# Layer two of a graph block: the edge rows are scaled by one VectorE product a batch, in place of sixteen ScalarE scalings

## The chip, the cores and the metric

One core of one Trainium2 chip runs the whole program. A core has five engines, each with an instruction stream of its own: TensorE (PE), VectorE (DVE), ScalarE (ACT), GpSimd (POOL) and SyncE (SP). They meet through semaphores only. The metric is the device time of one execution, in microseconds (us).

## The reference

A block on 6250 nodes with 256 features: two layers of graph attention over 106250 edges, a linear attention beside them, and a mixture of eight experts behind. What matters here is the second graph layer, and what follows it:

```python
def gat_conv(x, W, attn_l, attn_r, src, dst, n_nodes):     # layer two: H = 1, D = 256
    feat = (x @ W).reshape(n_nodes, H, D)
    e = jax.nn.leaky_relu(el[src] + er[dst], NEG_SLOPE)
    m = jax.ops.segment_max(e, dst, num_segments=n_nodes)
    ex = jnp.exp(e - m[dst])
    denom = jax.ops.segment_sum(ex, dst, num_segments=n_nodes)
    alpha = ex / denom[dst]
    return jax.ops.segment_sum(alpha[:, :, None] * feat[src], dst, num_segments=n_nodes)
...
    h = jnp.einsum('bfd,edh->bfeh', x, W1) + b1             # eight experts, three layers each
    h = jax.nn.relu(_bn(h, g1, be1, m1, v1))
    h = jnp.einsum('bfeh,ehk->bfek', h, W2) + b2
    h = jax.nn.relu(_bn(h, g2, be2, m2, v2))
    y = jnp.einsum('bfeh,ehd->bfed', h, Wo) + bo
    return jnp.einsum('bfed,fe->bfd', y, w)
```

Each edge's source row `feat[src]` is multiplied by a weight `ex` of its own and added to the sum of its destination.

## The kernel before

The program runs five passes: nodes, indices, the edges of layer one (with the linear attention beside them), the hidden pass between the layers, and the edges of layer two (with the experts beside them). The functions are the same for both layers; a `Layer` gives the numbers. Layer two has one head (`H` = 1) of 256 columns (`W` = `dim` = 256).

**Edges.** They are sorted by destination and laid out on 128 lanes. A *row* is one edge on each lane; 16 rows (`G`) are a *batch*, and a layer has 52 batches (`NB`). `rows` holds three batches in layer two: for each row 256 features, and in column `W` the score, later the weight.
- GpSimd gathers: one indirect DMA a row (`e_rows<-scratch_table,k_src`, L1349). It may write batch n only when the same row of batch n - 3 has been summed (`summed`).
- VectorE's `head(n + 1)` (L1399 to L1418) makes the score differences `d` of the next batch. It stands in batch n's code ahead of row 14, and needs all 16 gathers of batch n + 1.
- ScalarE takes the exp of `d` into `wr` (L1473) and into column `W` of `rows` (L1474), both at the start of batch n's code, behind everything it does in batch n - 1. Then it scales row after row in place (L1481) and signals each (`scaled`).
- VectorE sums: L1437 and L1441 for row 0, L1458 for rows 1 to 15, each on the one before (`ring`). In L1458 both the row and the running sum are inputs. Half batches of `ring` are stored by SyncE.

**Experts.** Work on nodes, four blocks of 121 at a time, is woven into the same code by the batch and the row: four batches are a *round*, and in it TensorE takes its group of nodes through the eight experts, two a batch. For expert e its program has the first layer of e + 1 (L2090, into `p_a`), the second of e (L2102, into `p_b`), the outputs of e - 1 (L2116, into `p_y`). ScalarE empties `p_a` and `p_b` into `h1`, `h2` by L2025, which stands in its code at rows 2, 5, 9 and 12 of a batch (in the fourth batch of a round partly at 8, 10 and 13). VectorE adds `p_y` to `y` by L1878 at rows 1 and 2 for one expert and at rows 8 and 9 for the next; TensorE's outputs of an expert wait until those of the expert before it have been added. In the first batch of a round VectorE also runs the scans of the tails (L1129, L1132) at row 3, for which TensorE waits with L1138; in its third it joins the sums of a finished group (from L1898 on; the shares and the first join at row 7, behind ScalarE's exp L2062).

Layer one has eight heads; ScalarE scales four of them, and VectorE the other four in one product a batch (L1427), 128 x 16 x 256 elements too, whose weights a copy of the exps in PSUM gives (`shared`). Layer two fills all of PSUM with the experts' banks and the tails' and has no `shared`.

Of the kernel before, what the change touches and what calls it, by code (L numbers as in the profile page):

```python
# [8 lines left out]
ALU = mybir.AluOpType  # L9
# [3 lines left out]
P = 128  # L13
# [6 lines left out]
G = 16  # L20
# [39 lines left out]


L1 = Layer("l1", 8, 512, 4, 2, 12)
L2 = Layer("l2", 1, 256, 1, 3, 14)


def wait(eng, sem, value):
# [1192 lines left out]
def edge_pass(nc, a, k, L, work_of):  # L1259
    H, W, R, dim, AH = L.heads, L.width, L.row, L.dim, L.act_heads  # L1260
# [3 lines left out]
    with Scope(nc, "e" + L.name[1]) as s:  # L1264
# [5 lines left out]
        rows = s.sb("rows", [P, B, G, L.table])  # L1270
# [13 lines left out]
        scaled, summed = s.sem("scaled"), s.sem("summed")  # L1284
# [1 line left out]
        stored = s.sems("stored")  # L1286
        tails = Tails(nc, a, k, L, s, tails_out)
        work = work_of(nc, a, k, s, tails, stored)
        shared = [s.ps(f"shared{i}", [P, 512]) for i in range(2)] if AH < H else None
        shared_ready = s.sem("shared_ready")  # L1290

        def share(b):
# [63 lines left out]
        def _(dve):  # L1356
            c = Steps(dve, step)
# [63 lines left out]
            for n in range(NB):  # L1421
                b, rb = n % 2, n % B
                dve.wait_ge(wr_ready, n + 1)
                if AH < H:
                    dve.wait_ge(shared_ready, n + 1)
                    v = rows[:, rb, :, AH * dim:W].rearrange("p j (h e) -> p j h e", h=H - AH)
                    c(nc.vector.tensor_tensor(v, v, broad(share(b)[:, AH:H, 1:G1].rearrange("p h j -> p j h"), dim), ALU.mult))  # L1427

                wait(dve, stored[0], n * 16)
                wait(dve, summed, n * G)  # L1430
                if AH < H:
                    c(nc.vector.tensor_tensor(ring[:, 0, 0, 0:W].rearrange(by_head, h=H),
                                              ring[:, 1, LENGTH[1] - 1, 0:W].rearrange(by_head, h=H),
                                              broad(share(b)[:, :, 0], dim), ALU.mult))
                    c(nc.vector.tensor_tensor(ring[:, 0, 0, W:W + H], ring[:, 1, LENGTH[1] - 1, W:W + H], wr[:, b, :], ALU.mult))
                else:
                    c(nc.vector.tensor_scalar(ring[:, 0, 0, 0:W + H], ring[:, 1, LENGTH[1] - 1, 0:W + H], wr[:, b, 0:1], None,  # L1437
                                              ALU.mult))
                c.done()
                dve.wait_ge(scaled, n * G + 1)  # L1440
                nc.vector.tensor_tensor(ring[:, 0, 0, 0:W + H], ring[:, 0, 0, 0:W + H], rows[:, rb, 0, 0:W + H], ALU.add  # L1441
                                        ).then_inc(summed, 1)

                for i, (c0, c1) in enumerate(HALVES):
                    if i == 1:
                        wait(dve, stored[1], n * 16)
                    for j in range(max(c0, 1), c1):
                        if j == L.ahead and n < NB - 1:
                            head(n + 1)
                        er_along(n, j)  # L1450
                        tails.vector(dve, n, j)
                        work.vector(dve, n, j)
                        if j == G - 1 and n:
                            wait(dve, tails.kept, n // PB)
                        prev = ring[:, i, j - c0 - 1, 0:W + H] if j > c0 else ring[:, 1 - i, LENGTH[1 - i] - 1, 0:W + H]
                        dve.wait_ge(scaled, n * G + (j + 1))
                        dve.wait_ge(summed, n * G + j)
                        nc.vector.scalar_tensor_tensor(ring[:, i, j - c0, 0:W + H], prev, k.same[:, n * G + j:n * G + j + 1],  # L1458
                                                       rows[:, rb, j, 0:W + H], ALU.mult, ALU.add).then_inc(summed, 1)
# [3 lines left out]
        def _(act):  # L1463
            work.scalar_first(act)
            act.wait_ge(er_ready, 1)
            for n in range(NB):
                b, rb = n % 2, n % B
                act.wait_ge(d_ready, n + 1)
                wait(act, summed, (n - 1) * G)
                if AH < H:  # L1470
                    nc.scalar.activation(shared[b][:, 0:H * G1], d[:, :, :].rearrange("p h j -> p (h j)"), ACT.Exp  # L1471
                                         ).then_inc(shared_ready, 1)
                nc.scalar.activation(wr[:, b, :], d[:, :, 0], ACT.Exp).then_inc(carry_ready, 1)  # L1473
# [3 lines left out]
                for i, (c0, c1) in enumerate(HALVES):  # L1477
                    for j in range(c0, c1):
                        for h in range(AH):
                            at = slice(h * dim, (h + 1) * dim)  # L1480
                            last = nc.scalar.activation(rows[:, rb, j, at], rows[:, rb, j, at], ACT.Copy,  # L1481
                                                        scale=rows[:, rb, j, W + h:W + h + 1])
                        last.then_inc(scaled, 1)
                        tails.scalar(act, n, j)
                        work.scalar(act, n, j)
                    wait(act, stored[i], n * 16)
                    nc.scalar.copy(ring[:, i, 0:c1 - c0, L.max:R],
                                   mext[:, b, :, 1 + c0:1 + c1].rearrange("p h j -> p j h")).then_inc(dm_ready[i], 1)
# [794 lines left out]
```

## Time and profile before

| | us |
|---|---|
| median of three timed runs | 3574.6 (3569.72 to 3576.8) |
| the profiled execution, its time | 3602.09 |
| its span, from the first instruction to the last | 3600.3 |
| mean granted TensorE clock over the span | 0.752 of full |

The profile is of one execution. The page gives, for each engine, its busy time over the span; the trace behind it gives every instruction with its start, its length, how long the engine had stood idle before it, and what ended that idle time. Layer two's batches run from 1987.7 us to the end of the gathers and sums near 3423; from then on TensorE works off the last experts.

### The profile page before, as it was taken

The page shows a single profiled execution, that of the slowest core. Times are in us where ns is not written, and L with a number is a line of the kernel's source. Part 1 is how long each engine was busy: PE and PEld are TensorE (multiplying, and loading weights), DVE is VectorE, ACT ScalarE, POOL GpSimd, SP SyncE. Part 2 cuts the span into 40 slices and gives each one's busy share as a digit, 9 for nine tenths or more (in the row PEclk, how much of TensorE's full clock was granted, in tenths as well). Part 3 has the DMA queues.
Part 4 walks back from the last instruction along what each step waited for, and adds up shares of the span by engine and source line. Part 5 has one row for each costly group of instructions (what it writes and reads, how often), then busy time and mean ns, then how long its engine had stood idle before and what let it go on. Part 6 is the DMA issues. An engine that isn't in the chain of part 4 may idle for free. (4 is left out here: it accounts for less than half of the span.)

```text
span 3600.3 us, 33860 instructions
## 1 busy us (share of the span) xinstructions
PE 2150.5 (60%) x7289; PEld 1354.6 (38%) x7289; DVE 2346.6 (65%) x5584; ACT 1911.7 (53%) x6229; POOL 2178.0 (60%) x2067
## 2 busy tenths in 40 slices
PE   6700555554554444443664004788888878878999
PEld 5600333332332333332443002444554445544565
DVE  6872788887888888786775244555565545655732
ACT  3301888787877767675443223544554445544632
POOL 2337677666777767673775766666666666666300
PEclk9855667666656655555887556899989989989999
DMA  6414899998999999996554475555555555555410
GB/s 219 125 21 121 324 359 351 338 334 329 353 351 375 361 327 371 333 373 247 152 142 99 142 234 166 161 170 183 188 159 170 178 165 184 171 159 181 151 36 12
DMA packets 249058, 793.62 MB, mean 220 GB/s; under 512 B 72064, under 2 KB 120035, under 8 KB 222197
## 3 DMA queue, kind: packets, MB, share of 16 engines
q0 software_dynamic: 132448, 379.32, 33.9%
q1 hardware_dynamic: 86327, 391.15, 28.6%
q10 hardware_dynamic: 30078, 20.99, 2.3%
q8 instruction: 59, 0.97, 0.1%
q14 instruction: 146, 1.20, 0.1%
HBM read 414.03 MB, written 378.16 MB: 220 GB/s over the span
## 5 line engine op out<-in xcount | busy, mean ns | idle before, releaser
L1349 POOL DMA_INDIRECT e_rows<-scratch_table,k_src x1664 | 1745.1, 1049 | 837.4 <-issue 397.8
L1458 DVE SCALAR_TENSOR_TENSOR e_ring<-e_ring,k_same,e_rows 128x520 f32<-128x520 f32 (+1 forms) x1560 | 968.0, 621 | 458.5 <-ACT e_rows L1481 177.0
L1481 ACT ACTIVATE e_rows<-e_rows 128x64 f32<-128x64 f32 (+1 forms) x4160 | 1199.8, 373 | 35.0 <-issue 29.9
L2116 PE MATMUL e_p_y<-e_wfo,e_h 128*121 128x256 f32 x1664 | 414.4, 404 | 135.3 <-DVE e_y L1878 117.4
L2116 PEld LDWEIGHTS e_p_y<-e_wfo,e_h 128*121 128x121 f32 x1664 | 323.4, 197 | 242.0 <-issue 124.2
L2090 PE MATMUL e_p_a<-e_xt,e_wf 128*128 128x484 f32 x832 | 383.9, 607 | 22.5 <-ACT e_xt L2040 11.7
L2025 ACT ACTIVATE e_h<-e_p_a,e_shift,e_scale 128x484 f32<-128x484 f32 x208 | 151.7, 750 | 448.1 <-remote 295.0
L1878 DVE SCALAR_TENSOR_TENSOR e_y<-e_p_y,e_w,e_y 121x256 f32<-121x256 f32 x416 | 181.3, 478 | 304.2 <-remote 105.9
L2102 PE MATMUL e_p_b<-e_h,e_wf 128*128 128x484 f32 x832 | 360.0, 572 | 7.9 <-issue 7.4
L1427 DVE TENSOR_TENSOR e_rows<-e_rows,e_shared 128x4096 f32<-128x4096 f32 x52 | 229.7, 4418 | 18.7 <-ACT e_shared L1471 7.5
L971 PE MATMUL e_p_kv<-e_wkv,nd_feat 128*121 128x512 f32 x208 | 184.6, 1039 | 92.0 <-DVE nd_feat L876 62.8
L2090 PEld LDWEIGHTS e_p_a<-e_xt,e_wf 128*128 128x128 f32 x832 | 168.7, 205 | 186.4 <-issue 160.6
L2025 ACT ACTIVATE e_h<-e_p_b,e_shift,e_scale 128x484 f32<-128x484 f32 x208 | 151.2, 749 | 148.4 <-PE e_p_b L2102 66.2
L2102 PEld LDWEIGHTS e_p_b<-e_h,e_wf 128*128 128x128 f32 x832 | 153.1, 190 | 176.5 <-issue 171.6
L1007 PE MATMUL e_p_q<-k_ident,e_low 121*128 121x121 f32 x104 | 33.1, 418 | 294.1 <-DVE e_low L902 253.1
L985 PE MATMUL e_p_c<-e_vext,e_kphi 121*128 121x129 f32 x208 | 62.5, 394 | 191.8 <-ACT e_low L938 99.9
L1123 PE MATMUL e_p_x<-k_ident,e_fin 128*8 128x128 f32 (+1 forms) x26 | 8.1, 313 | 203.9 <-ACT e_fin L1118 197.1
L1473 ACT ACTIVATE e_wr<-e_d 128x8 f32<-128x8 f32 (+1 forms) x104 | 21.4, 205 | 204.1 <-DVE e_d L1418 98.7
L1007 PEld LDWEIGHTS e_p_q<-k_ident,e_low 121*128 121x128 f32 x104 | 15.7, 207 | 299.3 <-DVE e_low L902 256.4
L1675 PE MATMUL hi_p_f<-hi_w,hi_ht 128*121 128x272 f32 x416 | 122.4, 445 | 0.1
L985 PEld LDWEIGHTS e_p_c<-e_vext,e_kphi 121*128 121x128 f32 x208 | 44.7, 266 | 200.3 <-ACT e_low L938 106.6
L971 PEld LDWEIGHTS e_p_kv<-e_wkv,nd_feat 128*121 128x121 f32 x208 | 57.9, 308 | 159.0 <-issue 87.1
(405 smaller groups left out, 3589.8 us busy)
## 6 DMA issues: line engine op xcount, KB each, us to landing
scratch_sums<-e_ring SPq DMA_DIRECT2D x104, 2112.0 KB
scratch_sums<-e_ring SPq DMA_DIRECT2D x104, 1032.0 KB
e_rows<-scratch_table,k_src POOLq DMA_INDIRECT x1664
scratch_table<-na_frow ACTq DMA_DIRECT2D x52, 245.8 KB
scratch_table<-hi_frow ACTq DMA_DIRECT2D x52, 124.8 KB
na_x<-in_x SPq DMA_DIRECT2D x13, 484.0 KB
e_wkv<-in_x SPq DMA_DIRECT2D x52, 121.0 KB
scratch_res<-e_wkv SPq DMA_DIRECT2D x52, 121.0 KB
```

The costliest lines, as they stand in the source:

```text
L971: nc.tensor.matmul(self.p_kv[0:BK, :], self.k.feat[:, t, kt, :], self.wkv[:, kt, :], start=kt == 0, stop=kt == 1)
L985: last = nc.tensor.matmul(self.p_c[:, m * (P + 1):(m + 1) * (P + 1)], part[0:BK, m * P:(m + 1) * P], self.vext[:, m, :], start=False, stop ...
L1349: nc.gpsimd.indirect_dma_start(out=rows[:, n % B, g, :], out_offset=None, in_=table, in_offset=bass.IndirectOffsetOnAxis(ap=k.src[:, n * G ...
L1427: c(nc.vector.tensor_tensor(v, v, broad(share(b)[:, AH:H, 1:G1].rearrange("p h j -> p j h"), dim), ALU.mult))
L1458: nc.vector.scalar_tensor_tensor(ring[:, i, j - c0, 0:W + H], prev, k.same[:, n * G + j:n * G + j + 1], rows[:, rb, j, 0:W + H], ALU.mult, ...
L1481: last = nc.scalar.activation(rows[:, rb, j, at], rows[:, rb, j, at], ACT.Copy, scale=rows[:, rb, j, W + h:W + h + 1])
L1675: last = nc.tensor.matmul(p_f[b][0:BK, 0:D + 16], ht[:, b, kt, :], w2[:, kt, :], start=kt == 0, stop=kt == 3)
L1878: last = nc.vector.scalar_tensor_tensor(y, self.p_y[bank][0:BK, i % 2 * D:(i % 2 + 1) * D], self.w[:, i, e:e + 1], y, ALU.mult, ALU.add)
L2025: self.nc.scalar.activation(h[:, e % 2, mt, :], p[mt][:, 0:GN], ACT.Relu, bias=self.shift[:, layer, 2 * e + mt:2 * e + mt + 1], scale=self ...
L2090: last = nc.tensor.matmul(self.p_a[mt][:, 0:GN], self.wf1[:, e, kt, mt * P:(mt + 1) * P], self.xt[:, kt, :], start=kt == 0, stop=kt == 1)
L2102: last = nc.tensor.matmul(self.p_b[mt][:, 0:GN], self.wf2[:, e, kt, mt * P:(mt + 1) * P], self.h1[:, e % 2, kt, :], start=kt == 0, stop=kt ...
L2116: last = nc.tensor.matmul(self.p_y[bank][0:BK, i * D:(i + 1) * D], self.h2[:, e % 2, kt, v:v + BK], self.wfo[:, e, kt, :], start=kt == 0, ...
```

## The change

`act_heads` of layer two goes from 1 to 0. The branch for it scales a whole batch with one TENSOR_TENSOR on VectorE, all 16 x 256 columns of a lane, whose second operand is the weight column of the same tile, repeated over 256 columns. It reads both operands in SBUF and stands at the head of the batch, behind the wait for the exps. ScalarE has no scaling and signals none, and VectorE's waits for `scaled` are gone. `shared` stays out in layer two, and layer one is as before.

```diff
-L2 = Layer("l2", 1, 256, 1, 3, 14)
+L2 = Layer("l2", 1, 256, 0, 3, 14)
...
-        shared = [s.ps(f"shared{i}", [P, 512]) for i in range(2)] if AH < H else None
+        shared = [s.ps(f"shared{i}", [P, 512]) for i in range(2)] if 0 < AH < H else None
...
                 dve.wait_ge(wr_ready, n + 1)
-                if AH < H:
+                if AH == 0:
+                    c(nc.vector.tensor_tensor(rows[:, rb, :, 0:W], rows[:, rb, :, 0:W], rows[:, rb, :, W:W + 1].to_broadcast([P, G, W]),
+                                              ALU.mult))
+                elif AH < H:
                     dve.wait_ge(shared_ready, n + 1)
...
-                if AH < H:
+                if 0 < AH < H:
                     c(nc.vector.tensor_tensor(ring[:, 0, 0, 0:W].rearrange(by_head, h=H),
...
                 c.done()
-                dve.wait_ge(scaled, n * G + 1)
+                if AH:
+                    dve.wait_ge(scaled, n * G + 1)
...
-                        dve.wait_ge(scaled, n * G + (j + 1))
+                        if AH:
+                            dve.wait_ge(scaled, n * G + (j + 1))
...
-                if AH < H:
+                if 0 < AH < H:
                     nc.scalar.activation(shared[b][:, 0:H * G1], d[:, :, :].rearrange("p h j -> p (h j)"), ACT.Exp
...
-                        last.then_inc(scaled, 1)
+                        if AH:
+                            last.then_inc(scaled, 1)
```

In VectorE's stream, at the passage from the first to the second batch of a round (batches 32 and 33), the program had these rows before: the last of `head`, the last two sums of the batch, then row 0 of the next (L1437, L1441) and the adds to `y`.

```order
3523 L1417 TENSOR_TENSOR e_d<-e_eext,e_mext 128x1
3524 L1418 TENSOR_TENSOR e_d<-e_eext,e_mext 128x16
3525 L1458 SCALAR_TENSOR_TENSOR e_ring<-e_ring,k_same,e_rows 128x257 x2
3526 L1437 TENSOR_SCALAR e_ring<-e_ring,e_wr 128x257
3527 L1441 TENSOR_TENSOR e_ring<-e_ring,e_rows 128x257
3528 L1878 SCALAR_TENSOR_TENSOR e_y<-e_p_y,e_w,e_y 121x256 x2
3529 L1458 SCALAR_TENSOR_TENSOR e_ring<-e_ring,k_same,e_rows 128x257
```

After the change the same place reads as follows, with the line numbers of the changed file (L1463 is the sum, L1440 and L1445 row 0, L1884 the add to `y`).

```order
3556 L1417 TENSOR_TENSOR e_d<-e_eext,e_mext 128x1
3557 L1418 TENSOR_TENSOR e_d<-e_eext,e_mext 128x16
3558 L1463 SCALAR_TENSOR_TENSOR e_ring<-e_ring,k_same,e_rows 128x257 x2
3559 L1425 TENSOR_TENSOR e_rows<-e_rows 128x16x256
3560 L1440 TENSOR_SCALAR e_ring<-e_ring,e_wr 128x257
3561 L1445 TENSOR_TENSOR e_ring<-e_ring,e_rows 128x257
3562 L1884 SCALAR_TENSOR_TENSOR e_y<-e_p_y,e_w,e_y 121x256 x2
```

One row is new, the product L1425, ahead of row 0's sum and the adds; nothing else changes its place.

ScalarE's stream at the same passage before: the end of batch 32 with its scalings (L1481) between the banks (L2025), then the exps of batch 33 (L1473, L1474).

```order
2226 L1487 COPY e_ring<-e_mext 128x8
2227 L1481 ACTIVATE e_rows<-e_rows 128x256 x2
2228 L2025 ACTIVATE e_h<-e_p_a,e_shift,e_scale 128x484 x2
2229 L1481 ACTIVATE e_rows<-e_rows 128x256 x3
2230 L2025 ACTIVATE e_h<-e_p_b,e_shift,e_scale 128x484 x2
2231 L1481 ACTIVATE e_rows<-e_rows 128x256 x3
2232 L1487 COPY e_ring<-e_mext 128x8
2233 L1473 ACTIVATE e_wr<-e_d 128x1
2234 L1474 ACTIVATE e_rows<-e_d 128x16
```

And after the change (L2031 empties a bank, L1478 and L1479 are the exps):

```order
2013 L1493 COPY e_ring<-e_mext 128x8
2014 L2031 ACTIVATE e_h<-e_p_a,e_shift,e_scale 128x484 x2
2015 L2031 ACTIVATE e_h<-e_p_b,e_shift,e_scale 128x484 x2
2016 L1493 COPY e_ring<-e_mext 128x8
2017 L1478 ACTIVATE e_wr<-e_d 128x1
2018 L1479 ACTIVATE e_rows<-e_d 128x16
```

The scalings are gone, and the exps follow the last bank behind one small copy.

## Rows read from the trace of the kernel before

**Rows 1.** The page: span, and busy time of each engine.

```profile
span 3600.3 us, 33860 instructions
PE 2150.5 (60%) x7289; PEld 1354.6 (38%) x7289; DVE 2346.6 (65%) x5584; ACT 1911.7 (53%) x6229; POOL 2178.0 (60%) x2067
```

**Rows 2.** Table of stretches: batches 0-7, 12-47, 48 to end; columns as headed.

```profile
core 0: us, PE busy (x) PEld busy (x) DVE busy (x) ACT busy (x) POOL busy (x), PEclk, DMA share, GB/s
1987.70:2213.20 225.50, 15.38 (x48) 9.07 (x49) 86.39 (x259) 63.21 (x174) 156.48 (x157) 0.51 0.58 185
2330.60:3338.90 1008.30, 838.37 (x2639) 493.75 (x2639) 572.12 (x1738) 501.69 (x1126) 653.34 (x657) 0.90 0.56 173
3338.90:3600.30 261.40, 251.38 (x842) 152.04 (x840) 111.38 (x317) 106.31 (x198) 33.41 (x33) 0.99 0.20 65
```

**Rows 3.** Groups, 2330.6 to 3338.9: busy us, mean ns | idle before <-releasers.

```profile
L1349 POOL DMA_INDIRECT e_rows<-scratch_table,k_src x577 | 569.5, 987 | 330.9 <-DVE e_ring L1458 167.1 <-issue 154.0 <-DVE e_ring L1441 8.6
...
L1138 PE MATMUL e_p_x<-k_ident,e_chain 1*128 1x1 f32 x9 | 2.0, 222 | 5.3 <-DVE e_chain L1132 5.3
```

**Rows 4.** Timeline in layer one: start, us, engine, instruction [idle before <-releaser].

```profile
597.46 4.42 DVE L1427 TENSOR_TENSOR e_rows<-e_rows,e_shared 128x4096 f32<-128x4096 f32 x1
598.56 0.95 POOL L1349 DMA_INDIRECT e_rows<-scratch_table,k_src  x1 [0.30 <-issue]
599.81 0.95 POOL L1349 DMA_INDIRECT e_rows<-scratch_table,k_src  x1 [0.30 <-issue]
```

**Rows 5.** Who waited for whom, 2330.6 to 3338.9: us, times, longest.

```profile
ACT e_h L2025 <- remote: 300.2, 52, 22.2
...
DVE e_ring L1458 <- ACT e_rows L1481: 103.3, 64, 9.4
PE e_p_y L2116 <- DVE e_y L1878: 102.4, 19, 15.2
```

**Rows 6.** Timeline, third batch of a round (batch 34), three engines.

```profile
2930.53 3.41 PE L2090 MATMUL e_p_a<-e_xt,e_wf 128*128 128x484 f32 x8
...
2952.51 0.95 POOL L1349 DMA_INDIRECT e_rows<-scratch_table,k_src  x1 [0.30 <-issue]
2956.89 1.40 ACT L2025 ACTIVATE e_h<-e_p_a,e_shift,e_scale 128x484 f32<-128x484 f32 x2 [22.23 <-remote]
...
2959.47 1.14 POOL L1349 DMA_INDIRECT e_rows<-scratch_table,k_src  x1 [6.01 <-DVE e_ring L1458]
```

**Rows 7.** Timeline, passage from a round's first to its second batch (32 to 33).

```profile
2910.57 1.40 ACT L2025 ACTIVATE e_h<-e_p_b,e_shift,e_scale 128x484 f32<-128x484 f32 x2 [6.39 <-remote]
2911.86 1.30 ACT L1481 ACTIVATE e_rows<-e_rows 128x256 f32<-128x256 f32 x3
...
2914.30 0.21 ACT L1474 ACTIVATE e_rows<-e_d 128x16 f32<-128x16 f32 x1
...
2915.58 0.94 POOL L1349 DMA_INDIRECT e_rows<-scratch_table,k_src  x1 [1.48 <-DVE e_ring L1458]
...
2916.05 0.87 DVE L1878 SCALAR_TENSOR_TENSOR e_y<-e_p_y,e_w,e_y 121x256 f32<-121x256 f32 x2
...
2917.06 1.31 PE L2116 MATMUL e_p_y<-e_wfo,e_h 128*121 128x256 f32 x5 [0.59 <-DVE e_y L1878]
```

**Rows 8.** Timeline of VectorE in batch 0 of layer two, two sums.

```profile
1996.56 0.49 DVE L1458 SCALAR_TENSOR_TENSOR e_ring<-e_ring,k_same,e_rows 128x257 f32<-128x257 f32 x1 [0.91 <-DVE e_ring L1458]
1997.96 0.49 DVE L1458 SCALAR_TENSOR_TENSOR e_ring<-e_ring,k_same,e_rows 128x257 f32<-128x257 f32 x1 [0.91 <-DVE e_ring L1458]
```

**Rows 9.** Timeline in the index pass: a VectorE product and GpSimd's scatters.

```profile
235.99 1.89 DVE L751 TENSOR_TENSOR at_diag<-k_ident,at_own 128x1664 f32<-128x1664 f32 x1
236.99 1.78 POOL L412 DMA_INDIRECT scratch_starts<-nd_er,k_index  x1 [0.31 <-issue]
...
239.08 1.02 POOL L412 DMA_INDIRECT scratch_starts<-nd_er,k_index  x1 [0.30 <-issue]
```

**Rows 10.** Timeline, third batch of a round and its passage to the fourth (34, 35).

```profile
2959.13 0.19 ACT L2062 ACTIVATE e_gsc<-e_gd 121x8 f32<-121x8 f32 x1
...
2961.43 0.49 DVE L1458 SCALAR_TENSOR_TENSOR e_ring<-e_ring,k_same,e_rows 128x257 f32<-128x257 f32 x1 [1.05 <-ACT e_rows L1481]
2961.84 0.16 DVE L1907 TENSOR_TENSOR e_gq<-e_grow,e_gsc 121x8 f32<-121x8 f32 x1
...
2979.14 0.87 DVE L1878 SCALAR_TENSOR_TENSOR e_y<-e_p_y,e_w,e_y 121x256 f32<-121x256 f32 x2
...
2980.16 3.69 PE L2116 MATMUL e_p_y<-e_wfo,e_h 128*121 128x256 f32 x16 [1.55 <-DVE e_y L1878]
```

**Rows 11.** Timeline, a round's first batch (36): exps, tails' scan, who waits.

```profile
3003.20 0.41 ACT L1118 COPY e_fin<-e_ring 128x258 f32<-128x258 f32 x1 [0.68 <-DVE e_ring L1458]
3003.63 1.28 ACT L1473 ACT_TABLE_LOAD   x1
...
3009.03 0.41 DVE L1132 TENSOR_TENSOR_SCAN e_chain<-k_break,e_chain 1x128 f32<-1x128 bf16 x1
...
3010.66 0.22 PE L1138 MATMUL e_p_x<-k_ident,e_chain 1*128 1x1 f32 x1
```

## The prediction

> **What bounds the kernel now.** I read the page first: no engine is full over the span [rows 1]. The change is in layer two alone, so the next view is the table of stretches, cut where layer two's batches begin and end [rows 2]. Its middle stretch holds batches 12 to 47, nine rounds of four in 1008.3 us: 112.0 us a round, 28.0 a batch. In it TensorE is busy for 838.4 us, 93.2 a round, at a mean granted clock of 0.90; GpSimd 653.3 us in 657 gathers; VectorE 572, ScalarE 502. The last stretch, from batch 48 to the end, is TensorE's own (251 of 261 us), so what the middle loses or gains arrives at the end.
>
> GpSimd needs a sum of its own. The groups of instructions give a gather of `rows` a mean of 0.987 us [rows 3], and each is followed by 0.30 us of issue time, as between the gathers in [rows 4]. 653.3 + 657 x 0.30 = 850.4 us, so **GpSimd has 94.5 us of work in a round of 112.0** and waits for the other 17.5, nearly all for VectorE's sums that free a buffer [rows 3]. VectorE waits for ScalarE's scaled rows (103.3 us) and TensorE for VectorE's adds to `y` (102.4 us, 11.4 a round) [rows 5]. The largest wait of all is ScalarE's for TensorE's first-layer banks, 300 us. One of these shows what it is [rows 6]: ScalarE stands idle for 22.2 us although the matmuls that fill its bank were recorded more than 20 us earlier, and goes on at 2956.89, 3.4 us after the last gather of an unbroken run of GpSimd's (2915.58 [rows 7] to 2953.46) ended; GpSimd itself had stopped only because it was three batches ahead. So long unbroken runs of gathers hold up the signals between the others, and a pause of GpSimd frees them. The opening of the layer looks the same: there one row follows the other on VectorE at 1.40 us for a row of 0.49, by its own semaphore [rows 8].
>
> **The change part by part.** *Removed:* 832 scalings on ScalarE, 16 a batch. One has 0.50 us on the page but they follow at 0.40 (three in 1.30 [rows 7]): 6.5 us a batch off ScalarE. What VectorE waited for them is gone too: 103.3 us over nine rounds [rows 5].
>
> *Added:* 52 products over 128 x 4096 float32 on VectorE. The same size stands in layer one: 4.42 us [rows 4]; 52 x 4.42 = 230 us of VectorE's work. VectorE then has (572 + 36 x 4.42) / 36 = 20.3 us a batch of 28.0: it doesn't become the bound. But the product stands whole ahead of the batch's first sum and of the first adds to `y`, where the sixteen scalings were spread over the batch.
>
> *What the product does to GpSimd.* Layer one's product reads its weights in PSUM, and gathers beside it take their usual 0.95 us [rows 4]. The new one reads both operands in SBUF. For that the trace has a case in the index pass: a TENSOR_TENSOR with both inputs in SBUF ran from 235.99 for 1.89 us; the scatter issued at 236.99, 1.02 us when alone, took 1.78 and ended 0.89 after the product [rows 9]. It had stood still until the product was through. A product of 4.42 us then holds GpSimd for 4.42 less what passes before the next gather would start, which is anything from 0 to 1.29, on average 0.64: 3.8 us a batch, 15.1 a round. GpSimd's work becomes 94.5 + 15.1 = 109.6 us a round, still under 112.0. That is a floor: whatever ScalarE's relief brings, a round can gain no more than 2.4 us while this holds.
>
> The Trainium skill ("SBUF — State Buffer", section "Who interferes with whom") says both things of this case: that a VectorE instruction with two SBUF inputs contends with a GpSimd one that reads SBUF, and that a probe of `tensor_tensor` did not stall DMAs issued by GpSimd, since writing descriptors needs the other half of the shared ports. By the second the floor would stay at 94.5 us. The rows side with the first, so I take 109.6.
>
> *The adds to `y`, batch by batch of a round.* The product delays the adds behind it unless VectorE arrives earlier by as much.
> - Second batch [rows 7]: ScalarE's bank is emptied at 2911.97, then come three scalings, a copy and the exps, whose weights are there at 2914.5; the add to `y` starts at 2916.05 and TensorE, which waited for it, at 2917.06. Without scalings the weights are there at about 2912.4, the product ends at 2916.8, the two ring instructions take 0.7: 2917.6, **1.5 us later**.
> - Fourth batch [rows 10]: TensorE waited 1.55 us for the add that began at 2979.14. VectorE had worked without a gap since 2961.84, where its row ended a wait for ScalarE of 1.05 us. What it needs there is ScalarE's exp of 2959.13, which itself stands behind two scalings; without any it could start at 2958.7, 3.1 us earlier: 4.4 - 3.1 = **1.3 us later**.
> - First batch [rows 11]: the exps follow a table load at 3003.63, which waits for the last two rows; they come 1.3 us earlier, the adds and the scan of the tails 3.1 later. TensorE waits for that scan (5.3 us over nine rounds [rows 3]) with 1.2 us to spare in the round shown and 0.1 to 2.1 in the nine, read pair by pair in the same way, 0.7 on average: **2.4 us later**.
> - Third batch: here is the long stall of [rows 6]; the product lies inside it and costs nothing. If the stall weren't there it would cost up to 4.4. But the product also is a pause of GpSimd in the middle of its run, and may free the signals earlier. Bounds: nothing, or all of TensorE's 11.4 us of waiting. The pause comes once, early in the run, and the run goes on behind it: I take a third, **4 us earlier**.
>
> Together 1.5 + 1.3 + 2.4 - 4 = +1.2 us a round, over the ten rounds from batch 8 to 47 +12 us.
>
> *Opening, batches 0 to 7* (225.5 us [rows 2]). GpSimd's work: 156.5 + 157 x 0.30 + 8 x 3.8 = 234, 8.5 us over today's. VectorE's side: eight products, 35 us at most, against rows that come at 1.40 us and might come faster behind a pause [rows 8]. I take +6, from -5 to +30.
>
> *End:* products sit beside a full TensorE; 0 to +4, taken as 0. Loads, stores, order of gathers and layer one are untouched.
>
> Sum: 12 + 6 = +18 us. The profiled execution took 3602.1 us, 27.5 more than the median of the timed runs; its sum is 3620, the median's 3574.6 + 18 = **3593 us**. A measurement of this kernel tells about 0.2% (7 us) from no change.
>
> **The rivals.**
> - *GpSimd's pauses take the place of its waits (faster).* If the pause frees the signals as soon as I think and TensorE loses its 11.4 us of waiting, the round falls until GpSimd's floor stops it: at most 2.4 us x 10 = 24 us, of which 8 to 24 arrive: 3550 to 3567. For it: [rows 6], and that VectorE no longer waits for ScalarE. Against: TensorE waits for precisely the adds behind the product. It decides from a relief of more than 6 us in the third batch.
> - *A draw.* A relief near 5 us and a short opening: within 7 us of 3575.
> - *The pauses are added to the waits.* A stalled ScalarE delays the exps, hence the product, while GpSimd runs on to three batches ahead and stops as today; then 15.1 us a round come on top, half of it +75 us (3650), all of it +150. For it: the run of [rows 6] began at 2915.58 [rows 7] and the first matmuls held up are those of 2930.5, 15 us on, while a batch of gathers is 16 x 1.287 = 20.6 us. Against: GpSimd has 17.5 us of waiting which the pauses can use up.
> - *The gathers aren't held.* Then GpSimd's floor is 94.5 and TensorE's 93.2 is the next; VectorE's relief could bring 5 to 10 us a round: 3475 to 3525. Against it [rows 9].
>
> **How the numbers follow.** My own case (+8 to +50) 0.42; GpSimd's floor 0.24; the draw 0.18; pauses added 0.12; not held 0.04. Faster 0.28, within 0.2% 0.18, slower 0.54. The range leaves out the last case, most of the added pauses and a little of the floor case: 3552 to 3650. My case alone has 3583 to 3625.
>
> **What would show it.** In the changed profile: 52 products near 4.4 us; one gather or so beside each that takes 2 to 5.3 us, so that GpSimd's busy time in layer two is some 200 us higher; its waits for VectorE's sums down from 17.5 us a round to under 5; no wait for a scaled row; TensorE's wait for adds to `y` at the second and fourth batch longer by 1 to 2 us, the stall of the third shorter; a round of 112 to 114 us. I am wrong in mechanism if gathers beside the product keep 0.95 us, and wrong in size if the third batch's stall goes altogether or gets a companion in every batch.

## The result, and the profile after

The changed kernel takes **3666.5 us** (median of four, 3653.0 to 3671.6) where the kernel before takes 3575.7 (3569.7 to 3580.1) in the same comparison: a ratio of 1.0249, 95% interval 1.0215 to 1.0283, 91 us slower. I had predicted 3593, from 3552 to 3650. The direction was right, the size was not, and it lies outside the range.

The page's busy times, the counterpart of [rows 1]:

```profile
span 3651.2 us, 32354 instructions
PE 2149.0 (59%) x7289; PEld 1364.1 (37%) x7289; DVE 2562.3 (70%) x5636; ACT 1581.5 (43%) x5397; POOL 2319.1 (64%) x2067
```

The table of stretches at the same places of the program as [rows 2]:

```profile
core 0: us, PE busy (x) PEld busy (x) DVE busy (x) ACT busy (x) POOL busy (x), PEclk, DMA share, GB/s
1971.30:2208.40 237.10, 19.13 (x56) 10.72 (x57) 121.12 (x269) 13.00 (x46) 182.21 (x158) 0.52 0.56 180
2332.80:3390.10 1057.30, 824.90 (x2637) 495.80 (x2636) 721.30 (x1775) 274.03 (x549) 750.71 (x656) 0.89 0.52 165
3390.10:3651.20 261.10, 250.01 (x843) 151.36 (x841) 124.02 (x321) 80.66 (x133) 36.76 (x32) 0.99 0.19 61
```

The opening is 11.6 us longer, batches 8 to 11 (what lies between the first two rows) 7.0, the nine rounds 49.0 (117.5 us a round in place of 112.0), and the end has not moved (261.1 against 261.4). Layer two thus takes 1679.9 us in place of 1612.6: **+67**. The remaining 24 us of the timed difference of 91 lie in which executions were profiled: that of the changed kernel (3653.0) is the fastest of its four, 13 us under their median, and that of before (3602.1) is 26 us over its median, of which 16 lie ahead of layer two (it began at 1987.7 us against 1971.3) and 10 in it.

The groups of the product and the gathers, in batches 12 to 47 (for the gathers, compare [rows 3]):

```profile
L1349 POOL DMA_INDIRECT e_rows<-scratch_table,k_src x576 | 655.8, 1139 | 282.9 <-issue 144.0 <-DVE e_ring L1445 88.8 <-DVE e_ring L1463 41.6
...
L1425 DVE TENSOR_TENSOR e_rows<-e_rows 128x4096 f32<-128x4096 f32 x37 | 163.6, 4423 | 159.8 <-ACT e_rows L1479 126.9 <-issue 32.8
```

Who waited for whom there, the counterpart of [rows 5]:

```profile
ACT e_h L2031 <- remote: 179.2, 45, 11.0
...
DVE e_rows L1425 <- ACT e_rows L1479: 126.9, 10, 20.1
PE e_p_y L2122 <- DVE e_y L1884: 124.0, 16, 21.2
```

The longest of ScalarE's waits for a bank is 11.0 us in place of 22.2. But what the tables put down to "remote" (179.2 us for 300.2) comes back under the first-layer matmuls (172.5 for 50.6), 352 us for 351 in all. A new wait stands beside them: VectorE's product waits for ScalarE's exps, 127 us in ten waits, with the adds to `y` behind it. The timeline of the passage from the third to the fourth batch of a round (38 to 39) shows one:

```profile
3111.70 0.20 DVE L1408 TENSOR_TENSOR_SCAN e_fext<-e_rflat,e_eext 128x17 f32<-128x17 f32 x1 [1.22 <-DVE e_eext L1406]
...
3114.50 0.16 DVE L1417 TENSOR_TENSOR e_d<-e_eext,e_mext 128x1 f32<-128x1 f32 x1 [2.33 <-DMA hi_rows<-scratch_tails_a,k_index]
...
3115.33 0.21 ACT L1479 ACTIVATE e_rows<-e_d 128x16 f32<-128x16 f32 x1
...
3118.52 0.94 POOL L1349 DMA_INDIRECT e_rows<-scratch_table,k_src  x1 [0.30 <-issue]
3119.43 0.17 DVE L1945 TENSOR_SCALAR e_var<-e_mv 121x4 f32<-121x4 f32 x1 [4.40 <-remote]
...
3122.00 4.42 DVE L1425 TENSOR_TENSOR e_rows<-e_rows 128x4096 f32<-128x4096 f32 x1
...
3123.74 3.49 POOL L1349 DMA_INDIRECT e_rows<-scratch_table,k_src  x1 [0.84 <-DVE e_ring L1463]
...
3127.06 0.87 DVE L1884 SCALAR_TENSOR_TENSOR e_y<-e_p_y,e_w,e_y 121x256 f32<-121x256 f32 x2
3128.08 1.18 PE L2122 MATMUL e_p_y<-e_wfo,e_h 128*121 128x256 f32 x2 [18.99 <-ACT e_h L2031]
```

VectorE waits 1.2, 2.3 and 4.4 us for signals, one of them certainly its own (L1408 for L1406), while GpSimd gathers without a break; the gather of 3118.52 is the last of the run. Only then comes the product, which holds one of GpSimd's gathers (3.49 us), and behind it the adds. TensorE has stood still for 19.0 us.

### The profile page after: what moved, and what is told of

Same layout as the page of the kernel before. It is cut to its first block and busy times, and to the rows that moved or that the text cites. A ratio compares the mean times of both kernels' runs of the same rounds, so it can differ in the third digit from the quotient of the medians.

```text
span 3651.2 us, 32354 instructions
## 1 busy us (share of the span) xinstructions
PE 2149.0 (59%) x7289; PEld 1364.1 (37%) x7289; DVE 2562.3 (70%) x5636; ACT 1581.5 (43%) x5397; POOL 2319.1 (64%) x2067
## 5 line engine op out<-in xcount | busy, mean ns | idle before, releaser
L1349 POOL DMA_INDIRECT e_rows<-scratch_table,k_src x1664 | 1872.6, 1125 | 761.8 <-issue 387.3
L1463 DVE SCALAR_TENSOR_TENSOR e_ring<-e_ring,k_same,e_rows 128x520 f32<-128x520 f32 (+1 forms) x1560 | 966.5, 620 | 188.2 <-ACT e_rows L1486 54.4
L1486 ACT ACTIVATE e_rows<-e_rows 128x64 f32<-128x64 f32 x3328 | 829.5, 339 | 40.7 <-issue 27.3
L2122 PE MATMUL e_p_y<-e_wfo,e_h 128*121 128x256 f32 x1664 | 402.4, 398 | 189.3 <-DVE e_y L1884 148.4
L1425 DVE TENSOR_TENSOR e_rows<-e_rows 128x4096 f32<-128x4096 f32 x52 | 230.0, 4422 | 173.1 <-ACT e_rows L1479 126.9
L2031 ACT ACTIVATE e_h<-e_p_a,e_shift,e_scale 128x484 f32<-128x484 f32 x208 | 154.1, 754 | 424.6 <-PE e_p_a L2096 294.5
L1884 DVE SCALAR_TENSOR_TENSOR e_y<-e_p_y,e_w,e_y 121x256 f32<-121x256 f32 x416 | 180.9, 476 | 119.6 <-PE e_p_y L2122 101.8
L2031 ACT ACTIVATE e_h<-e_p_b,e_shift,e_scale 128x484 f32<-128x484 f32 x208 | 154.0, 751 | 225.8 <-PE e_p_b L2108 110.7
L1478 ACT ACTIVATE e_wr<-e_d 128x8 f32<-128x8 f32 (+1 forms) x104 | 21.1, 203 | 291.3 <-DVE e_d L1418 156.3
L218 POOL DMA_INDIRECT na_found<-in_dst,na_piece x52 | 54.8, 1054 | 98.1 <-DVE na_piece L270 98.1
```

Source lines behind the costliest of these rows:

```text
L1349: nc.gpsimd.indirect_dma_start(out=rows[:, n % B, g, :], out_offset=None, in_=table, in_offset=bass.IndirectOffsetOnAxis(ap=k.src[:, n * G ...
L1425: c(nc.vector.tensor_tensor(rows[:, rb, :, 0:W], rows[:, rb, :, 0:W], rows[:, rb, :, W:W + 1].to_broadcast([P, G, W]), ALU.mult))
L1884: last = nc.vector.scalar_tensor_tensor(y, self.p_y[bank][0:BK, i % 2 * D:(i % 2 + 1) * D], self.w[:, i, e:e + 1], y, ALU.mult, ALU.add)
L2031: self.nc.scalar.activation(h[:, e % 2, mt, :], p[mt][:, 0:GN], ACT.Relu, bias=self.shift[:, layer, 2 * e + mt:2 * e + mt + 1], scale=self ...
L2122: last = nc.tensor.matmul(self.p_y[bank][0:BK, i * D:(i + 1) * D], self.h2[:, e % 2, kt, v:v + BK], self.wfo[:, e, kt, :], start=kt == 0, ...
```

## The experiments

The comparisons fell on chips that differ in one respect, which the traces show: on some, signals are late as above; in the traces of the others none is. I call them the first kind (the result above; e1 to e4 on one chip; e13 to e15 on another) and the second (e5 to e8 on one chip; e9 to e12 on another). Each ratio is to the kernel before on the same chip.

| run | what | kind | median, us | ratio, 95% interval |
|---|---|---|---|---|
| after | the change | 1 | 3666.5 | 1.025 (1.022 to 1.028) |
| e1 | no product (rows unscaled) | 1 | 3587.3 | 1.003 (1.001 to 1.006) |
| e2 | one-input reduction (rows unscaled) | 1 | 3663.4 | 1.022 (1.016 to 1.027) |
| e3 | product in four parts | 1 | 3566.9 | 0.998 (0.996 to 1.001) |
| e4 | adds ahead of rows 3 to 15 | 1 | 3601.9 | 1.007 (1.004 to 1.009) |
| e5 | before, lead 2.5 batches | 2 | 3318.7 | 1.012 (1.010 to 1.014) |
| e6 | four parts, lead 2.5 | 2 | 3432.0 | 1.046 (1.044 to 1.048) |
| e7 | the change | 2 | 3472.1 | 1.058 (1.056 to 1.060) |
| e8 | sixteen TENSOR_SCALARs | 2 | 3314.0 | 1.009 (1.008 to 1.011) |
| e9 | before | 2 | 3281.2 | 1.000 (0.999 to 1.001) |
| e10 | one-input reduction (rows unscaled) | 2 | 3298.5 | 1.004 (1.003 to 1.006) |
| e11 | product in four parts | 2 | 3376.8 | 1.028 (1.025 to 1.030) |
| e12 | no product (rows unscaled) | 2 | 3288.2 | 1.001 (1.000 to 1.002) |
| e13 | before, lead 2.5 | 1 | 3597.2 | 1.000 (0.997 to 1.003) |
| e14 | sixteen TENSOR_SCALARs | 1 | 3640.8 | 1.011 (1.006 to 1.016) |
| e15 | the change | 1 | 3719.2 | 1.032 (1.026 to 1.037) |

The kernel before has medians of 3575.1 beside e1 to e4, 3282.2 and 3282.9 beside e5 to e12, and 3601.6 beside e13 to e15.

**e1, no product.**

```diff
-                if AH == 0:
-                    c(nc.vector.tensor_tensor(rows[:, rb, :, 0:W], ...
-                elif AH < H:
+                if 0 < AH < H:
```

> The changed kernel without its product, so that layer two's rows are summed unscaled (the scaling is left out). ScalarE has no scaling, VectorE has no product: what is left is ScalarE's relief alone. Theory A, that the 91 us come from the product (its hold of GpSimd, 3.8 us a batch, and the delay of what stands behind it): with both gone the time falls under the kernel before, 3480 to 3560 us, GpSimd's gathers keep 0.95 us and its waits return. Theory B, that they come from the signals that are held up during long unbroken runs of gathers, which are only pushed elsewhere once ScalarE's scalings no longer pace the kernel: 3560 to 3640 us, TensorE's and ScalarE's long waits stay in each round. If it is under 3560 the product alone is to blame, if it is over 3600 the product is to blame for less than half.

3587 us. Of the 91 us, 79 go with the product, and what is left is slower than before, not faster: to take 6.5 us a batch off ScalarE, and all waits for scaled rows off VectorE, is worth nothing. Batches 12 to 47 take 111.8 us a round against 112.0:

```profile
2309.50:3315.50 1006.00, 845.88 (x2638) 491.50 (x2637) 571.67 (x1737) 272.98 (x549) 650.87 (x656) 0.90 0.56 173
```

**e2, a reduction with one input in SBUF.**

```diff
-                    c(nc.vector.tensor_tensor(rows[:, rb, :, 0:W], rows[:, rb, :, 0:W], ...
+                    c(nc.vector.tensor_reduce(total[:, :], rows[:, rb, :, 0:W], AX.X, ALU.add))
```

> The changed kernel with a TENSOR_REDUCE over the same 128 x 16 x 256 elements in place of the product (one input in SBUF, 16 results a lane; the scaling of the rows is left out). VectorE is occupied as long as by the product, near 4.3 us, at the same place, but has only one large input in SBUF. If the hold of GpSimd is the price (theory of the hold), gathers beside it keep 0.95 us, GpSimd's busy time falls by 130 to 140 us, and the kernel by most of the loss: 3570 to 3620 us. If the price is that the adds to y stand behind 4.4 us of VectorE (theory of the path), the time stays at 3650 to 3670 us although the gathers are free. If gathers beside a reduction are held too, the run says nothing between them.

The stretch of batches 12 to 47 of e2, two groups in it and TensorE's wait for the adds:

```profile
2321.90:3394.30 1072.40, 874.30 (x2632) 509.96 (x2631) 722.37 (x1775) 273.44 (x548) 650.26 (x656) 0.87 0.52 162
L1350 POOL DMA_INDIRECT e_rows<-scratch_table,k_src x576 | 566.2, 983 | 401.9 <-DVE e_ring L1445 142.0 <-issue 135.9 <-DVE e_ring L1463 124.0
...
L1426 DVE TENSOR_REDUCE e_total<-e_rows 128x16 f32<-128x4096 f32 x37 | 163.4, 4417 | 137.2 <-ACT e_rows L1479 118.4 <-issue 18.8
...
PE e_p_y L2122 <- DVE e_y L1884: 73.6, 21, 7.4
```

The reduction is as long as the product (4.42 us) and the gathers are free (0.983 us a piece as in [rows 3]), yet the time is 3663 us. On this kind of chip **the hold of GpSimd costs nothing** that can be told from zero (the two intervals leave room for some 20 us); GpSimd merely waits longer. From e1 to e2, 76 us, is the price of 4.4 us of VectorE at the head of the batch. It isn't all waiting for the adds: that wait (73.6 us, 7.4 at most) is less than in the kernel before (102.4). TensorE's busy time is 28 us longer than in e1 too, at a mean granted clock of 0.87 against 0.90.

**e3, four parts.**

```diff
-                    c(nc.vector.tensor_tensor(rows[:, rb, :, 0:W], ...
+                    product(n, 0, 4)
...
+                        if AH == 0 and j % 4 == 0:
+                            product(n, j, j + 4)
+                            c.done()
```

> The changed kernel with its product cut into four of four rows each (128 x 4 x 256, near 1.15 us), ahead of the sums of rows 0, 4, 8 and 12. VectorE's work and the time with two inputs in SBUF are the same, but no adds stand behind more than 1.15 us of it. Theory of the hold: GpSimd is held for 4 x (1.15 less 0.5) = 2.6 us a batch or more in place of 3.8, so 3650 to 3670 us, at best 12 us less. Theory of the path: the adds of the second, fourth and first batch come 3.3 us earlier, and a round loses 3 to 5 us, over ten rounds 30 to 50 us: 3610 to 3640 us.

3567 us: the whole loss is gone, more than either theory gave.

```profile
2306.50:3300.50 994.00, 845.78 (x2641) 494.15 (x2640) 733.62 (x1882) 274.24 (x549) 705.72 (x656) 0.90 0.57 175
```

A part takes 1.22 us, VectorE has slightly more work than with the whole product (733.6 us in the nine rounds against 721.3), and GpSimd is still held: 705.7 us against 650.9 in e1. What cost was neither work nor hold but the size of the block. One thing here stays open: e3 is 20 us faster than e1, which does less. So differences of that size on this kind of chip can't be split into shares of work. TensorE's waits for the adds in batches 12 to 47 of e3, 124.0 us and up to 21.2 in the changed kernel and 102.4 in [rows 5], shrink to:

```profile
PE e_p_y L2129 <- DVE e_y L1891: 33.6, 9, 7.4
```

**e4, the adds first.**

```diff
-                    c(nc.vector.tensor_tensor(rows[:, rb, :, 0:W], ...
+                    product(n, 0, 3)
...
+                        if AH == 0 and j == 3:
+                            product(n, 3, G)
+                            c.done()
```

> The changed kernel with its product cut in two: rows 0 to 2 at the head of the batch (near 0.85 us), rows 3 to 15 (near 3.6 us) behind the first adds to y and the tails' first scan, ahead of the sum of row 3. The hold of GpSimd stays nearly whole (3.6 less 0.6, and 0.85 less 0.4: 3.4 us a batch). Theory of the hold: 3650 to 3670 us. Theory of the path: what a round loses by late adds at rows 1 and 2 (1.5 us in the second, 1.3 in the fourth, 2.4 in the first batch by my steps) comes back, 52 us over ten rounds: 3600 to 3635 us.

3602 us, inside what the path theory gave: 65 of the 91 us come back although the large product (3.62 us) and most of the hold remain.

```profile
2318.70:3335.90 1017.20, 851.89 (x2639) 499.71 (x2638) 730.49 (x1810) 275.85 (x549) 728.75 (x657) 0.91 0.55 171
```

With e3 this shows that it is a large block at the head of the batch that costs. What behind it bears the cost isn't shown: the edit puts the sums of rows 0 to 2, the first adds and the tails' first scan ahead of the large product all at once.

**e5 and e13, a shorter lead for GpSimd,** and **e6,** the same edit on e3.

```diff
-                    wait(pool, summed, (n - B) * G + g + 1)
+                    wait(pool, summed, (n - B) * G + g + 1 + (8 if B == 3 else 0))
```

> The kernel before, with GpSimd's gathers of layer two held 8 rows further back: they wait for the sum 8 rows later, so that GpSimd gets at most 2.5 batches ahead in place of 3. Nothing else is changed. Theory of the runs (signals between the engines are held up while GpSimd gathers without a break, and come when it stops): GpSimd stops some 8 x 1.29 = 10 us sooner in the third batch of a round, the long wait of 20 to 25 us there falls to 10 to 15, and up to 5 us a round come back: 3520 to 3565 us. Rival (the long wait has nothing to do with the run, and GpSimd only lost lead): the long wait stays, GpSimd waits more elsewhere and a round gets longer: 3580 to 3640 us.

> The kernel with the product in four parts (3566.9 us), with the same shorter lead of 2.5 batches. Theory of the runs: as for the kernel before, 3510 to 3560 us, and the long wait of the third batch (19.5 us in its trace) halved. Rival: 3570 to 3630 us, the long wait stays.

These two were meant for late signals and fell on a chip that has none. There the shorter lead only costs: 1.2% by itself, and 3432 us against 3377 (e11) on the four parts. On the first kind it was run again:

> The kernel before with GpSimd's lead cut from 3 to 2.5 batches, as in e5, which fell on a chip of the second kind (no late signals) and lost 1.2% there. In the traces of the first kind VectorE's waits for its own semaphore in head() were late only in runs of gathers of 25 us and more or just behind one, never in the first 20 us of a run. On a chip of the first kind, by the theory of the runs: a shorter lead ends the run sooner, the longest wait of ScalarE in the third batch falls from 22 to under 15 us and the kernel gains, 3520 to 3565 us; by the rival (lead is only lost): 3590 to 3640 us. On a chip of the second kind: 1.012 times the kernel before again.

The wait of ScalarE for the first-layer banks there, to be held against 300.2 us and 22.2 in [rows 5]:

```profile
ACT e_h L2025 <- remote: 250.7, 48, 15.4
```

The longest wait falls from 22.2 to 15.4 us, nearly as the theory of the runs wants, but the time stays (1.000): GpSimd's own waits for sums rise from 167 to 183 us, and the round is 111.6 us against 112.0. That long runs go with late signals holds; that shortening them pays doesn't.

**e7, the changed kernel on the second kind, and e9, the kernel before.**

> The changed kernel once more, on the same chip as the others of this call, for a second profile. The two profiled executions differ by 51 us, the medians by 91. If layer two of the changed kernel varies from run to run, this profile has a layer two longer than 1680 us, by up to 20; if what varies lies ahead of layer two, layer two has 1675 to 1685 us again and starts later than 1971. Time 3650 to 3675 us.

> The kernel before, for a profile beside the others of this call. The last call ran on another chip than the first: there the kernel before took 3282 us in place of 3575, and in the traces of its variants VectorE's waits for its own semaphore were 34 ns each, where the first chip shows up to 4.9 us. If this call's chip is of the second kind: a round near 96 us (GpSimd's own 94.5 plus little), no wait put down to a remote signal, and about 3282 us. If it is of the first kind: 3575 us, a round near 112 us, some 300 us of such waits.

Batches 12 to 47 of e9 (table of stretches, and GpSimd's group):

```profile
2171.60:3018.80 847.20, 798.37 (x2639) 480.31 (x2638) 569.44 (x1738) 502.68 (x1126) 647.02 (x658) 0.97 0.66 206
L1349 POOL DMA_INDIRECT e_rows<-scratch_table,k_src x578 | 564.4, 977 | 176.1 <-issue 137.7 <-DVE e_ring L1458 38.1 <-DVE e_ring L1441 0.3
```

And of e7:

```profile
2218.30:3197.70 979.40, 819.13 (x2638) 490.86 (x2637) 722.21 (x1775) 274.16 (x550) 779.23 (x658) 0.89 0.57 178
L1349 POOL DMA_INDIRECT e_rows<-scratch_table,k_src x578 | 672.7, 1164 | 176.1 <-issue 136.2 <-DVE e_ring L1463 39.9
```

In both, the idle time before a gather is 176.1 us for 578, the 0.30 us of issue each and nothing more: GpSimd never waits. Its busy time plus 658 x 0.30 is 844 us of 847 in e9 and 977 of 979 in e7. It is the bound, the round is its work, and the change lengthens the round from 94.1 to 108.8 us because GpSimd is held (779.2 - 647.0) / 37 = 3.6 us a product. The passage of the timeline that was shown above looks like this in e7:

```profile
2952.98 0.20 DVE L1408 TENSOR_TENSOR_SCAN e_fext<-e_rflat,e_eext 128x17 f32<-128x17 f32 x1
...
2953.49 0.16 DVE L1417 TENSOR_TENSOR e_d<-e_eext,e_mext 128x1 f32<-128x1 f32 x1
...
2955.12 4.42 DVE L1425 TENSOR_TENSOR e_rows<-e_rows 128x4096 f32<-128x4096 f32 x1
...
2955.74 4.62 POOL L1349 DMA_INDIRECT e_rows<-scratch_table,k_src  x1 [0.30 <-issue]
...
2961.20 2.03 PE L2122 MATMUL e_p_y<-e_wfo,e_h 128*121 128x256 f32 x4 [7.49 <-DVE e_y L1884]
```

The same instructions, no wait for an own signal, the product 1.6 us behind `d` (L1417) in place of 7.5, and one gather that is let go when the product ends. One way by which the 14.7 us reach TensorE stands in the table of waits of e7: VectorE's join in the third batch waits for its gathers (`e_grow`), which come behind the others on GpSimd, and ScalarE's exp behind it, with its later banks:

```profile
ACT e_gsc L2068 <- DVE e_gd L1906: 182.4, 9, 21.4
DVE e_gm L1904 <- DMA e_grow<-scratch_tails_b,e_index: 166.0, 9, 19.6
```

In e9 the same two waits are:

```profile
DVE e_gm L1898 <- DMA e_grow<-scratch_tails_b,e_index: 77.2, 9, 10.1
ACT e_gsc L2062 <- DVE e_gd L1900: 74.6, 9, 9.9
```

**e10, e11, e12: the reduction, the four parts and no product on the second kind.**

> The changed kernel with the reduction of the same 128 x 4096 elements in place of the product (the scaling is left out), as in e2, where it changed nothing (3663 against 3666 us). On a chip of the second kind GpSimd never waited in the changed kernel's rounds (108.8 us, its work with the pauses 109.6), so the hold should be the price: with free gathers the round falls to 96 to 100 us and the kernel from 3472 to 3300 to 3350 us. If the block in front of the adds is the price there too, it stays over 3420 us. On a chip of the first kind: 3650 to 3670 us again.

> The product in four parts, with the usual lead, as in e3. On a chip of the second kind the pauses stay in part (in e6 GpSimd's gathers were held 9 us a round, against 16 with the whole product), so it is slower than the kernel before, by 60 to 120 us: 3340 to 3400 us. If it is as fast as the kernel before, the block and not the hold is what costs. On a chip of the first kind: 3560 to 3580 us again.

> The changed kernel without its product (the scaling is left out), as in e1. On a chip of the second kind, where no signal is late, ScalarE's relief should show: GpSimd's work of 94.5 us a round and TensorE's 93 are the floor, so 3230 to 3282 us. If the kernel before is already at that floor, it stays within 10 us of it. On a chip of the first kind: 3580 to 3595 us again.

Batches 12 to 47 of e10, then of e12, then of e11:

```profile
2178.00:3028.50 850.50, 795.51 (x2638) 481.32 (x2637) 723.53 (x1774) 275.54 (x550) 650.54 (x657) 0.96 0.66 205
```

```profile
2172.50:3023.70 851.20, 799.66 (x2638) 479.04 (x2637) 572.24 (x1737) 274.14 (x549) 651.31 (x657) 0.97 0.66 204
```

```profile
2207.50:3119.60 912.10, 822.61 (x2639) 488.75 (x2638) 732.50 (x1883) 275.20 (x549) 711.91 (x658) 0.94 0.62 191
```

Here the order of the first kind is turned round. With free gathers the block of 4.4 us costs 10 us (3299 against 3288 without product): of the 190 us, 173 are **the hold**. Four parts, which lost nothing on the first kind, lose 2.8%: 711.9 + 658 x 0.30 = 909 us of 912, again GpSimd's own work. ScalarE's relief is worth nothing here either, since GpSimd is full.

**e8 and e14, one TENSOR_SCALAR a row, issued one row ahead of its sum.**

```diff
+                c(nc.vector.tensor_scalar(rows[:, rb, j, 0:W], rows[:, rb, j, 0:W], rows[:, rb, j, W:W + 1], None, ALU.mult))
...
+                            dve.wait_ge(c.sem, c.base + c.n - (1 if j + 1 < G else 0))
```

> The changed kernel with the product cut into sixteen TENSOR_SCALARs of one row (128 x 256), each issued one row ahead of its sum. One large input in SBUF each. By the table of groups a TENSOR_SCALAR over 257 columns takes 0.35 us: 5.6 us of VectorE a batch in place of 4.4, but no block ahead of the adds. If only the block in front of the adds mattered, it is as fast as the four parts: 3555 to 3580 us. If the smaller hold of GpSimd in four parts matters too (its busy time was 77 us over that of the kernel before), this one is faster still, 3540 to 3560 us. If VectorE's extra work matters: 3580 to 3620 us.

> Sixteen TENSOR_SCALARs of one row each, as in e8 (1.009 times the kernel before, on a chip of the second kind). On a chip of the first kind, if the block of 4.4 us in front of the adds is what cost 76 us there (e1 against e2), it is as fast as the four parts or no product: 3560 to 3590 us. If VectorE's work itself costs (it has 1.2 us a batch more than the product): 3600 to 3670 us. On the second kind: 1.009 times the kernel before again.

0.354 us a row in the groups, 5.7 us a batch, one large input: hardly a hold (on the second kind GpSimd has 671.4 us in the nine rounds against 647.0) and no block. Of the forms that scale the rows it is the mildest on the second kind (1.009), and it loses 1.1% on the first, where the four parts lose nothing. So the size of the block isn't the whole account there. What was expected beforehand of such a time, VectorE's extra work, doesn't explain it: the pieces add up to 0.8 us a batch more than the four parts (5.7 against 4 x 1.22), but they overlap their neighbours, and VectorE is busy for 705.4 us in the nine rounds of e14 against 733.6 in e3. It fell on another chip of that kind, where the changed kernel loses more too (e15); why it loses stays open.

**e15, the changed kernel once more on the first kind.**

> The changed kernel once more. On a chip of the first kind: ratio 1.02 to 1.03, and a second profile of it there, whose layer two is 1680 us if the 24 us by which the medians differ more than the profiled pair lie ahead of layer two or in the profiled run of the kernel before, 1690 to 1700 us if they lie in layer two of the changed kernel. On a chip of the second kind: ratio 1.058 again, a round of 108.8 us.

3719 us on a chip where the kernel before takes 3602: a ratio of 1.032, a little over what was expected. Layer two takes 1717.5 us in its trace, 121.7 a round, over both values expected and 38 us more than in the first trace. In the traces of before and of e13, which take the same time as each other in a comparison, layer two has 1612.6 and 1613.0 us. So the price of the change varies between two chips of this kind: 91 and 118 us by the medians, 67 and 104 in layer two of these single traces. No version here beats the kernel before on either kind.

## Why the prediction missed

- **The product**: 52 at 4.42 us, as said.
- **The hold**: right in mechanism and in size. On the second kind 51 of the 52 products hold one gather, for up to 5.2 us, and it ends 0.8 to 0.9 us behind the product, as the scatter of [rows 9] did; the hold is 3.6 us a product for the 3.8 that I gave. The round of 109.6 us that I gave as GpSimd's floor is 108.8 on the second kind, where the floor is reached. On the first kind only 41 products catch a gather (GpSimd's busy time +141 us over the span, where I had said some 200), and by e2 they cost nothing that shows, as I had assumed below the floor. The Trainium skill ("SBUF — State Buffer", section "Who interferes with whom") says that a VectorE instruction with two SBUF inputs contends with a GpSimd instruction that reads SBUF, and that one with at most one, outside the 2-port modes, does not: by that rule e10 and e7 differ as they do, and the traces agree (gathers of 0.979 and 1.164 us on average). Its other sentence, that a probe of `tensor_tensor` did not stall DMAs from GpSimd, does not hold for these gathers: 4.62 us beside the product, 0.95 alone.
- **The third batch: this step failed.** I wrote that "the product lies inside it and costs nothing", that the pause of GpSimd frees the signals, and took "a third, **4 us earlier**". There is no relief. Counted by place in the round (first, second, third, fourth batch), from row 0's first instruction to that of the next batch, the means of the nine rounds are 23.9, 24.5, 38.5, 25.2 us before and 21.6, 21.1, 42.2, 32.5 after: the third batch is 3.7 us longer and the fourth 7.3, the other two shorter by 2.3 and 3.4. The third is long without any product too: e1 has 23.6, 19.2, 45.7 and 23.2. What the whole block adds to e1 stands in the fourth batch, 32.5 us here and 30.1 in e2, against 25.2 before, 23.2 in e1 and 21.7 in e3. The long wait came back at the passage to the fourth batch, in front of the product, where the exps, the product and the adds to `y` stand in one line behind a late signal. Without the 4 us my terms give 1.5 + 1.3 + 2.4 = 5.2 us a round, and the round got 5.4 longer, 49 us in nine. That agreement is luck, as the next point says.
- **The adds of the second, fourth and first batch**: I gave +1.5, +1.3 and +2.4 us and measured -3.4, +7.3 and -2.3. No term is right at its place; only their sum, with the third batch's +3.7, comes near, and from e1 to e2 (111.8 and 119.2 us a round) the block costs 7.4. That the loss comes from the block is shown by e3 and e4; that it comes by the adds is argued.
- **The opening**: +11.6 us for +6, within my bounds on this kind; on the second, 28 (224.7 against 196.7 in e9). Batches 8 to 11 lost 7.0 where I counted a round of 1.2. The second kind's 28 are near the bound of +30 and come from the hold: without product (e12) the opening takes 196.5 us there, with the reduction (e10) 199.8.
- **ScalarE's relief** had no term of its own, but I let it offset the delays. e1 and e12 give it nothing, on either kind.
- **The rival "pauses added to the waits"** held the measured time (3650 and more) by another mechanism: e2 has no pauses and the same time. I had left most of it out of the range.
- **The miss**: 73 us between 3593 and 3666. Of it 40 are that one guess over ten rounds, 6 the opening and 3 to 4 the rest of layer two; the other 24 are the two profiled executions, each off its median. By the guess alone the time would have come to 3633, inside the range still; with the other 33 it left it.

## What to carry to other kernels

A block of work put on an engine that is not full can cost what stands behind it in that engine's order. Try it in pieces: here four of 1.2 us in place of one of 4.4 gave back the whole loss where signals came late. A product of two SBUF operands on VectorE also stopped GpSimd's gathers here, and whether that shows depends on whether GpSimd waits anyway: compute its work per round first. And a measured ratio belongs to the chip it was taken on: the same edit lost 2.5 and 3.2% where signals came late and 5.8% where they did not, for different reasons.

## What the runs showed of the hardware

Signals between instructions, those of an engine to itself among them, are late on two of the chips here and not on the other two. In the second kind (e7, e9) VectorE's waits between L1406, L1408 and L1412 are nearly all 34 or 35 ns and never over 0.25 us. On the first kind, read pair by pair over the whole span of the kernel before, all 158 such waits within the first 20 us of an unbroken run of gathers are at most 35 ns, and of the 40 that lie more than 25 us into a run (one broken by no gap over 0.6 us) 7 are over 0.3 us, up to 1.22; in the changed kernel none of 108 and 13 of 90. So lateness goes with long runs of GpSimd's gathers (whether the run brings it about, or something that builds up beside it, no run tells), and the e4 trace, with runs of up to 104 us in its nine rounds and a round of 113.0, shows that their length alone doesn't set the price. Why the second kind is free of it, with GpSimd gathering without any pause, stays open. The kernel before has a granted clock of 0.97 in the nine rounds on the second kind, where TensorE is busy for 94% of them (e9), and of 0.90 on the first, where it is busy for 83%.
